# A first block with tokens on partitions, batch-norm statistics, folded weights and several batches in flight

## What is computed

```python
mod = (_silu(c) @ wmod).reshape(16, 6, 1, -1)
sa, ca, ga, sb, cb, gb = (mod[:, i] for i in range(6))
ga = (2 * (ga >= 0) - 1) * jnp.maximum(jnp.abs(ga), 0.25)      # gb likewise
h = _layernorm(x) * (1 + ca) + sa
x = x + ga * attn(h, Wqkv, bqkv, Wln, bln)
h = _layernorm(x) * (1 + cb) + sb
x = x + gb * six_layers(h, ...)

def attn(x, Wqkv, bqkv, Wln, bln):
    q, k, v = jnp.split(x @ Wqkv + bqkv, 3, axis=2)
    q = q - q.mean(axis=2, keepdims=True)
    k = k - k.mean(axis=2, keepdims=True)
    q2, k2 = q * q, k * k
    q2 = l2norm(q2 / (q2.sum(axis=2, keepdims=True) + 1e-7), axis=-1)
    k2 = l2norm(k2 / (k2.sum(axis=2, keepdims=True) + 1e-7), axis=-2)   # over tokens
    kv = jnp.einsum('bnc,bnd->bcd', k2, v)
    return (v + jnp.einsum('bnc,bcd->bnd', q2, kv) / math.sqrt(N)) @ Wln + bln
```

## Time and profile before

| | us |
|---|---|
| median of three runs (3974.95 to 3983.92) | 3975.99 |
| profiled execution | 3987.9 |
| its span, first to last instruction | 3986.1 |
| PE busy | 3633.8 (91%) |
| DVE busy | 2734.0 (69%) |
| ACT busy | 2766.0 (69%) |
| POOL busy | 1037.4 (26%) |

### The profile page before, as it was taken

How to read it: one execution, slowest core, us unless ns; L and a number is a source line. 1 busy time by engine, 2 the same in 40 slices (tenths; PEclk the granted TensorE clock), 3 DMA queues, 4 the chain that set the end, 5 groups by cost and what they waited for, 6 DMA issues and landing times.

```text
span 3986.1 us, 157311 instructions
## 1 busy us (share of the span) xinstructions
PE 3633.8 (91%) x64569; PEld 2525.9 (63%) x64761; DVE 2734.0 (69%) x5376; ACT 2766.0 (69%) x9073; POOL 1037.4 (26%) x857
## 2 busy tenths in 40 slices
PE   6776999999999999999999999999999999999997
PEld 3333666666666666666666666666666666666665
DVE  3334777777777777777777777777777777777774
ACT  3443776776777776777777677777777777777775
POOL 0001232232232233232223223223223223223220
PEclk7556999999999999999999999999999999999998
DMA  1001555445455445455545454545554545544452
GB/s 49 7 7 31 115 115 121 108 106 137 105 119 122 107 111 136 107 121 117 116 111 125 114 125 105 124 106 123 122 117 109 120 112 123 115 114 110 111 121 68
DMA packets 361465, 421.61 MB, mean 106 GB/s; under 512 B 52480, under 2 KB 266000, under 8 KB 360000
## 3 DMA queue, kind: packets, MB, share of 16 engines
q1 hardware_dynamic: 360768, 411.67, 44.8%
HBM read 19.30 MB, written 2.10 MB: 5 GB/s over the span
## 4 chain that ended last, share of the span: by engine, by line
PE 77%; ACT 9%; issue 5%; DVE 0%; SPq 0%; DMA 0%; POOL 0%; DVEq 0%; ACTq 0%
PE ring_ps L1062 18%; PE out_ps L1176 8%; PE ring_ps L1109 7%; PE score_ps L1127 7%; PE out_ps L1204 7%; PE out_ps L1164 7%; ACT probs L659 6%; PE turn_ps L1146 6%; PE turn_ps L1138 4%; PE small_ps L1073 4%; PE turn_ps L1211 2%; PE score_ps L1117 2%; ACT att_t L647 1%; ACT L641 1%; PE out_ps L1194 1%
## 5 line engine op out<-in xcount | busy, mean ns | idle before, releaser
L659 ACT ACTIVATE probs<-score_ps,neg_max,rq 128x64 f32<-128x64 f32 x3072 | 1191.7, 418 | 185.9 <-DVE neg_max L876 184.7
L838 DVE TENSOR_TENSOR prod<-ring_ps,tables 128x512 f32<-128x512 f32 x1536 | 951.4, 681 | 157.3 <-PE ring_ps L1062 146.5
L532 POOL TENSOR_TENSOR ks<-prod 128x1024 f32<-128x1024 f32 x192 | 451.5, 2352 | 2102.8 <-DVE prod L838 2018.6
L1062 PE MATMUL ring_ps<-xs,wqk 128*128 128x256 f32 x3072 | 765.7, 387 | 11.9 <-DVE xs L825 5.1
L614 ACT ACTIVATE square<-ring_ps,biases 128x512 f32<-128x512 f32 x768 | 507.1, 687 | 252.0 <-DVE prod L838 229.7
L659 ACT ACTIVATION_READ_ACCUMULATOR probs<-score_ps,neg_max,rq 128x1 f32 x3072 | 673.6, 219 | 0.0
L1062 PEld LDWEIGHTS ring_ps<-xs,wqk 128*128 128x128 f32 x3072 | 555.5, 191 | 116.3 <-issue 41.1
L647 ACT ACTIVATE att_t<-turn_ps 128x512 f32<-128x512 f32 x384 | 229.3, 597 | 501.0 <-PE turn_ps L1146 501.0
L532 POOL TENSOR_TENSOR qs<-prod 128x1024 f32<-128x1024 f32 x192 | 451.9, 2354 | 243.5 <-DVE prod L838 235.9
L1164 PE MATMUL out_ps<-v,pt 64*32 64x64 f32 x24576 | 349.7, 224 | 88.5 <-issue 87.1
L1109 PE MATMUL ring_ps<-wv,xs 128*128 128x512 f32 x768 | 405.5, 631 | 1.0 <-issue 1.0
(11 more groups left out here) (156 smaller groups left out, 4483.7 us busy)
## 6 DMA issues: line engine op xcount, KB each, us to landing
v<-vs SPq DMA_DIRECT2D x1344, 128.0 KB
qt<-qs SPq DMA_DIRECT2D x768, 128.0 KB
kt<-ks SPq DMA_DIRECT2D x768, 128.0 KB
v<-vs SPq DMA_DIRECT2D x192, 64.0 KB
wqk<-in_L_ffn_Wqkv SPq DMA_DIRECT2D x6, 1024.0 KB, 5.2
wv<-in_L_ffn_Wqkv SPq DMA_DIRECT2D x6, 512.0 KB
wo<-in_L_ffn_Wo SPq DMA_DIRECT2D x6, 512.0 KB
prod<-in_L_attn_x SPq DMA_DIRECT2D x16, 128.0 KB, 2.1
```

Of the source, the lines that this page charges most:

```text
L532: pool.tensor_tensor(dst, prod_a[p % 2], prod_b[p % 2], ALU.add).then_inc(rot_ready, 1)
L659: last = nc.scalar.activation(probs[i][:, j, e, :], score_ps[e][:, KEYS * j:KEYS * (j + 1)], ACT.Exp, bias=neg_max[:, h:h + 1], scale=rq[p ...
L838: last = V.tensor_tensor((prod_b if a else prod_a)[p % 2][:, f, :] .rearrange("p (u c) -> p u c", u=2), bank[:, :].rearrange("p (u c) -> p ...
L1062: last = mm(bank_of(s, parity)[:, TOKENS * f:TOKENS * (f + 1)], wqk[:, n, 2 * c + f, a, :], xs[:, WINDOW:PADDED], start=True, stop=True)
```

## The change

The first block is written anew; the layers' steps stay as they are.

- The input lands in `x1_all` with tokens on partitions, in five loads (before: one load of 128 KB a batch). The residual stays there.
- Each layernorm has its statistics from two BN_STATS and two BN_AGGR instructions on DVE (steps LS1, LS2), Ln and Exp of two columns on ACT (LR1, LR2), one tensor_scalar a tile (LX1, LX2), two transposes on PE (LT1, LT2) and one ACT instruction that applies scale and shift on the way out of PSUM (LH1, LH2).
- The q and k columns of the weight and the bias are centred once at the start, so that means fall away. The bias is split into three bf16 parts and added by a bf16 product with three rows.
- The value weight is multiplied by the output weight once (`v_ln`); POOL multiplies it and the bias by the gate of each batch (GW) and adds the bias to the residual (XB). kv is formed turned, multiplied by the output weight (KW) and gated (KG). The step Y gives the gated branch in four products, tokens on partitions, and X1 adds it to the residual.
- The square roots become Ln and Exp (RN); no other table is loaded in the block.
- The gates of all batches are spread over the partitions once, by 16 products and four copies, between the first and the second projection.
- `walk_first` walks lists in which each step has the number of batches that it is ahead: `QK:3` in a period is batch period + 3. There is no hardware loop.
- The bf16 constants are made by POOL. PE, ACT and DVE start after four loads (`cond_landed`).
- Output: 16 rounds of one batch with four buffers; ACT scales by the gate, PE turns, DVE adds the residual, SP writes 128 KB.

The two places of the order. First PE: the block's loop in the program before, from the projection on,

The core of the diff (added lines; what is taken out stands in the functions printed above):

```diff
+PE_FIRST = """
+Y:0 LT1:3 KV:1 QK:3 KW:1 QT:1 LT2:0 KC:2
+"""
+DVE_FIRST = """
+QE:0 LS1:3 LX1:3 MK:1 MX:1 X1:0 LS2:0 IV:2 NK:2 QF:1 LX2:0 KG:1
+"""
+ACT_FIRST = """
+LR1:3 SQ:2 LH1:3 LR2:0 KE:1 VT:2 RN:1 NQ:2 LH2:0
+"""
+POOL_FIRST = """
+GW:2 XB:2
+"""
...
+        def walk_first(order, step):
+            for period in range(-FIRST_AHEAD, BATCH):
+                for kind, ahead in order:
+                    if 0 <= period + ahead < BATCH:
+                        step(kind, period + ahead)
...
+        def qkv_bank(b, tile):
+            return (ring_ps, score_ps)[b % 2][tile]
...
+            load_x(0)
+            for dst, src in ((cond[:, :], t["L0_c"]), (biases[:, :], t["biases"]), (ident[:, :], t["ident"]),
+                             (wmod[:, :], t["L0_wmod"])):
+                sp.dma_start(dst, src).then_inc(cond_landed, 16)
...
+            for b in range(BATCH):
+                sp.wait_ge(e_out, at(b, 1, 1))
+                sp.dma_start(out_dram[:, b, :, :], x_out[b % 4].rearrange("p (t c) -> p t c", t=TILES)
+                             ).then_inc(out_landed[b % 4], 16)
...
+                if kind == "GW":
+                    pool.wait_ge(rows_kept, 4)
+                    pool.wait_ge(w_kept, 2)
+                    if b >= 1:
+                        pool.wait_ge(f_y, at(b - 1, 1))
+                    pool.wait_ge(f_xb, at(b, 1))
+                    pool.tensor_tensor(v_ln_b[b % 2][:, :], v_ln[:, :], gate_rows[:, b, :], ALU.mult)
+                    pool.tensor_tensor(bias_b[:, :], bias_y[:, :], gate_rows[:, b, :], ALU.mult).then_inc(f_gw, 1)
+                if kind == "XB":
+                    pool.wait_ge(f_gw, at(b, 1, 1))
+                    pool.wait_ge(lx[0], at(b, 1, 1))
+                    pool.tensor_tensor(tiles(b), tiles(b), bias_b[:, :].rearrange("p (o c) -> p o c", o=1)
...
+            def rsqrt(n, b):
+                act.wait_ge(la[n], at(b, 1, 1))
+                nc.scalar.activation(log_x[n][:, :], mean_var[n][:, :, 1], ACT.Ln, bias=ln_eps[:, :]
+                                     ).then_inc(log_made[n], 1)
+                act.wait_ge(log_made[n], at(b, 1, 1))
+                act.wait_ge(lx[n], at(b, 1))
+                nc.scalar.activation(rstd_x[n][:, :], log_x[n][:, :], ACT.Exp, bias=zero_col[:, :], scale=-0.5
+                                     ).then_inc(lr[n], 1)
...
+                if kind == "LH1":
+                    act.wait_ge(lt[0], at(b, 1, 1))
+                    act.wait_ge(c_mod_done, 1)
+                    if b >= 2:
+                        act.wait_ge(f_y, at(b - 2, 1))
+                    nc.scalar.activation(h0[b % 3][:, :], out_ps[0][:, 0:TOKENS], ACT.Identity, bias=mod[:, b, 0:1],
+                                         scale=mod[:, b, 1:2]).then_inc(lh[0], 1)
...
+                    last.then_inc(f_sq, 1)
+                    if b == 0:
+                        for four in range(4):
+                            act.wait_ge(rows_made, four + 1)
+                            nc.scalar.activation(gate_rows[:, 4 * four:4 * four + 4, :]
+                                                 .rearrange("p b c -> p (b c)"),
+                                                 (small_ps, out_ps[1])[four % 2][:, :], ACT.Copy).then_inc(rows_kept, 1)
...
+                if kind == "RN":
+                    act.wait_ge(f_max, at(b, 1, 1))
+                    act.wait_ge(f_kmax, at(b, 1, 1))
...
+                    nc.scalar.activation(log_n2[:, :], n2[:, :], ACT.Ln, bias=zero_col[:, :]).then_inc(f_log, 1)
...
+                        act.wait_ge(f_kg, at(b - 1, 1))
+                    nc.scalar.activation(r3[i][:, :], log_n2[:, :], ACT.Exp, bias=zero_col[:, :], scale=-0.5
+                                         ).then_inc(f_r, 1)
...
+            for b in range(BATCH):
+                act.wait_ge(x_ready, at(BATCH * (DEPTH - 1) + b, 1, 1))
+                if b >= 4:
+                    act.wait_ge(e_turned, at(b - 4, 1, 1))
+                nc.scalar.activation(x_fin[b % 4], x_all[:, columns(b)], ACT.Identity, bias=zero_col[:, :],
+                                     scale=mod[:, b, 5:6]).then_inc(e_fin, 1)
...
+                V.tensor_copy(bias_part[:, :], bias3[:, :]).then_inc(bias_done, 1)
+                dve.wait_ge(bias_done, n + 1)
+                if i < 2:
+                    V.tensor_tensor(bias3[:, :], bias3[:, :], bias_part[:, :], ALU.subtract)
+                if i == 0:
+                    V.tensor_scalar(sums3[0], bias_part[:, :], ident[0:3, 0:1], None, ALU.mult).then_inc(bias_done, 1)
+                else:
+                    V.scalar_tensor_tensor(out=sums3[i % 2], in0=bias_part[:, :], scalar=ident[0:3, i:i + 1],
+                                           in1=sums3[1 - i % 2], op0=ALU.mult, op1=ALU.add).then_inc(bias_done, 1)
+                dve.wait_ge(bias_done, n + 2)
+                n += 2
+            V.tensor_copy(bias_bf[:, :], sums3[0]).then_inc(bias_done, 1)
...
+                for tile in range(TILES):
+                    last = V.bn_stats(stats[n][:, tile, :], tiles(b)[:, tile, :])
+                last.then_inc(ls[n], 1)
...
+                    last = V.bn_aggr(mean_var[n][:, tile, :], stats[n][:, tile, :])
+                last.then_inc(la[n], 1)
+            def layernorm(n, b, dst):
+                dve.wait_ge(lr[n], at(b, 1, 1))
+                dve.wait_ge(lt[n], at(b, 1))
+                for tile in range(TILES):
+                    last = V.tensor_scalar(dst[:, tile, :], tiles(b)[:, tile, :], mean_var[n][:, tile, 0:1],
+                                           rstd_x[n][:, tile:tile + 1], ALU.subtract, ALU.mult)
+                last.then_inc(lx[n], 1)
...
+                if kind == "QF":
+                    dve.wait_ge(f_r, at(b, 1, 1))
+                    dve.wait_ge(f_qt, at(b, 1))
                     for tile in range(TILES):
+                        last = V.tensor_scalar(q_fin[:, tile, :], qk_sq[i][:, tile, 0, :], qk_inv[i][:, tile, 0:1],
+                                               r3[i][:, tile:tile + 1], ALU.mult, ALU.mult)
+                    last.then_inc(f_qfin, 1)
...
+                if kind == "KG":
+                    dve.wait_ge(f_kw, at(b, 1, 1))
+                    dve.wait_ge(f_r, at(b, 1, 1))
+                    dve.wait_ge(f_y, at(b, 1))
+                    dve.wait_ge(rows_kept, 4)
+                    V.scalar_tensor_tensor(out=kv_ln[:, :], in0=turn_ps[:, 0:DIM], scalar=r3[i][:, 2:3],
+                                           in1=gate_rows[:, b, :], op0=ALU.mult, op1=ALU.mult).then_inc(f_kg, 1)
+                if kind == "X1":
+                    dve.wait_ge(f_y, at(b, 1, 1))
+                    dve.wait_ge(f_xb, at(b, 1, 1))
+                    V.tensor_tensor(x1_all[:, columns(b)], small_ps[:, 0:TOKENS], x1_all[:, columns(b)],
+                                    ALU.add).then_inc(f_x1, 1)
+            walk_first(DVE_FIRST, first_step)
...
                     for tile in range(TILES):
+                        bank = qkv_bank(b, tile)[:, 0:3 * DIM]
+                        mm(bank, ones_bf[:, :], bias_bf[:, :], start=True, stop=False)
+                        last = mm(bank, h0[b % 3][:, P * tile:P * (tile + 1)], w0[:, :], start=False, stop=True)
+                    last.then_inc(f_qkv, 1)
+                    if b == 0:
+                        pe.wait_ge(c_clamped, 1)
+                        pe.wait_ge(c_mod_done, 1)
+                        pe.wait_ge(w_kept, 2)
+                        for four in range(4):
+                            if four >= 2:
+                                pe.wait_ge(rows_kept, four - 1)
+                            for r in range(4):
+                                row = 4 * four + r
+                                last = mm((small_ps, out_ps[1])[four % 2][:, DIM * r:DIM * (r + 1)],
+                                          ident[0:BATCH, row:row + 1].to_broadcast([BATCH, P]), gates[:, 0:DIM],
+                                          start=True, stop=True)
...
+                if kind in ("KC", "KV", "KW"):
+                    u, bu = first_user_before("K", kind, b)
+                    if u == "KC":
+                        pe.wait_ge(f_kmax, at(bu, 1, 1))
+                    if u == "KV":
+                        pe.wait_ge(f_kvt, at(bu, 1, 1))
+                    if u == "KW":
+                        pe.wait_ge(f_kg, at(bu, 1, 1))
...
+                if kind == "KC":
+                    pe.wait_ge(f_k2, at(b, 1, 1))
                     for tile in range(TILES):
+                        last = mm(turn_ps[:, 0:1], k_sq2[:, tile, :], qk_inv[i][:, tile, 1:2], start=(tile == 0),
+                                  stop=(tile == TILES - 1))
+                    last.then_inc(f_kcol, 1)
...
+                if kind == "KV":
+                    pe.wait_ge(f_v, at(b, 1, 1))
...
+                if kind == "Y":
+                    pe.wait_ge(f_kg, at(b, 1, 1))
+                    pe.wait_ge(f_qtc, at(b, 1, 1))
```

(8 more changed lines are left out.)

681 lines of the change are left out of this document (342 added, 339 removed).

## The result

The changed kernel takes **3778.28 us** (median of 4 runs, 3773.25 to 3782.35) against 3975.47 us (median of 4, 3973.96 to 3983.92) for the kernel before: ratio **0.9499**, interval 0.9482 to 0.9517. That is 197.2 us less.

A forecast was written before the change was run, and what follows sets the result against it. No engine is full; one batch's serial chain, 20.4 us, bounds the first block. Block ending at 188.5 instead of 357.0 saves 168.5 us, output 2.5: 3976 - 168.5 - 2.5 = 3805 us, range 3783 to 3834.

The forecast's parts named there:

- Where the time goes: Whole kernel: only start, first block and output can change; block and start 168.5 us less, output 2.5 less, layers nothing.
- layers unchanged within 5 us: Six layers after the first block: sign that their length stays at 3612.6 us from v2's clearing to the last x.
- Which clock?: PE in the first block: clock between slow and fast, mean near 0.7, so 9.5 us between batches.
- P: First block: time between two batches once the new pipeline is full, forecast at 9.5 us.
- the walk: First block: one period followed through the engines' lists from the end of KG, 7.9 us at the fast clock.
- Terms: First block, work a period: PE 11.0 us slow or 6.0 fast, ACT 6.5, DVE 5.6.
- The start: Before the pipeline is full: first statistics near 20.5 us, first full period from 47.7 us.
- The last three rows: End of the first block, where work runs out: periods of 6.5, 6 and 5 us.
- Rival 3: First block: three batches in flight do not come about, POOL slows DVE; 12 us a period, 3837.5 us, chance 0.12.
- Rival 4: First block: each period waits for one batch's whole chain, 24.3 us, slower than before at 3997 us; chance 0.02.
- The sum: First block ends at 65 us plus 13 periods, 188.5 us; with the output's 2.5 us off the median, 3805 us.
- rival 1: First block: PE's clock stays fast, 7.9 us a period, block ends at 167.7, time 3784 us; chance 0.16.

The follow-up runs named there:

- the bias pair: Changed kernel with projection bias as one-row fp32 products instead of three bf16 rows, 3807.36 us; the same with 128-row products in their place, 3786.85 us.
- its dose of 0.78 us: Changed kernel with four more batch-norm statistics a batch on DVE behind LS1, read by nobody: 3777.97 us, ratio 0.9475.

## Why the prediction was right or wrong

- **Where the time goes: right for block and output, open for the layers.** The block gave 193.4 us and the output 2.5, of 197.2 between the medians. The output's 2.5 us was read from the profile, not tested by itself, and it met the forecast by a slip: 3983.3 in the sum is 2.8 less than 3986.1, not 2.5. The sign "layers unchanged within 5 us" was missed: 3612.1 against 3597.8 in the two profiles. Kernels with the old block had 3603.6 to 3612.1, those with the new one 3586.8 to 3610.7, so this can be mere variation, and no run settles it. (A small misreading: in the earlier trace rows PE is at 9 tenths from the fifth slice on, not the fourth.)
- **The step that failed: "Which clock? I take the middle, P = 9.5."** The clock did not settle in the middle; it read 1.00 from 48 to 150 us, and P was 7.30. The middle cost 1.6 us a period, 21 us in 13 periods, and the walk's 0.6 us (next point) another 8, of which the last rows took back 3. Its evidence was the busy share, three quarters before and after, and "three quarters busy was not enough before". The share was forecast well (78%) and does not decide: the old loop at 76% read 0.55, and the bias pair had 86 and 85% and differed in the clock. What differs is how the busy time is laid out, PE's waits of up to 2.1 us in the old loop and at most 0.9 in the new one; filled so that they were 0.8, the old loop read 0.97. The rule weighed there, that PE kept free of long gaps stays fast (the Trainium skill, TensorE: Matmul & The Clock Gate, Why this matters for your kernels), gave the right rival; the trace agrees with it here, 1.00 from 48 to 150 us, and up to 145 us PE waits for nothing longer than 0.9 us. It is not the whole: in the kernel with one-row fp32 products the waits that the timeline shows are as short in most periods, and the clock was lost. Why that kernel loses it stays open.
- **The walk, P = 7.9 at the fast clock: right in form, 0.6 us too long.** QF waits for RN (1.17 us), LH2 for LX2, and ACT's row closes the ring. Measured from the end of KG (walk in brackets), at which each step ends: LX1 at 2.4 (2.5), X1 at 3.0 (3.3), LS2's statistics at 3.8 (4.15), RN at 5.9 (6.5), LX2 at 7.05 (7.5), KG at 7.3 (7.9). It is the sum of many small overestimates, the largest on ACT: 6.0 us busy a period, 6.5 in the sum.
- **Terms.** Statistics: two in 0.48 to 0.49, two aggregates in 0.25 with a mean of 166 ns, as taken. The bf16 bias product: 0.50 at the slow clock, 0.33 at the fast, where I took 0.4 between 0 and 0.8. PE at the fast clock 5.7 (6.0), DVE 5.3 (5.6). Evictions with pointer operands 0.57 (0.5).
- **The start: right.** First statistics 21.2 (20.5), first full period from 48.1 (47.7).
- **The last three rows: 20.7, not 17.5** (from 48.1 + 13 x 7.30 to 163.7). The clock fell as the pipeline emptied. With fillers and the clock at 1.00 they took 18.1 us (142.5 to 160.6).
- **Rival 3** (no three batches in flight, or POOL beside DVE) did not come. The contention is there, 0.32 us beside POOL and 0.17 without for the clamp of line 928, but DVE has room: its dose of 0.78 us cost nothing.
- **Rival 4's price was too high**: 20.4 us, not 24.3, for one batch at a time.
- **The sum** as it came out: 188.5 + 0.4 (start) - 28.6 (13 x 2.2) + 3.2 (last rows) = 163.5, measured 163.7. The range, from 3783, stopped just under rival 1 (3784), so that a chain a little shorter than that rival's walk fell outside.

## What to carry to other kernels

The gain here came with the depth of the overlap: cheaper instructions alone gave nothing, two batches 80 us, the full pipeline 197. Price a removed instruction by the structure it stands in: the same table loads were worth nothing in the serial loop and all of their length in the pipeline. Where TensorE's clock is in doubt, look at its single waits and at what its products are, not only at how long it is busy, and where two levels compete take one for the forecast and put the other wholly, with the error of its own chain, inside the range.

## What the chip showed that I had not expected

- The kind of product matters to the clock. With two one-row fp32 products a period, PE busy 86% of a fast period, the clock is lost again and again (0.86 over 40 us); with 128-row products in their place, busy 85%, it stays 1.00. In the old loop, filled, the same one-row products leave it at 1.00 in most batches. During 16-row products without a gap it was lost too (at 28.5 us).
- Two fp32 products of 384 columns start 0.84 us apart when one has one row and the other 128, and 0.64 apart when both have 128, both at the fast clock.
- Some 0.9 us more on ACT made the clock drop now and then for some 3 us, and a period of 7.7 us then took 8.9.
- In the slow serial loop a saving of some 0.6 us a batch went together with the loss of the batches that had run partly at the fast clock, and the block did not get shorter.
- 11.6 us less in the first block were followed by 10.6 us more in the same six layers. Other pairs show less, and why is open.
